# Expert second product as five f32r passes, ternary product in bf16, and five scatters to six gathers

## Chip, core and metric

The kernel runs on one core of a Trainium2 chip (trn2). The metric is the device time of one launch in microseconds. The engines named below: TensorE (PE in the profile), VectorE (DVE), ScalarE (ACT), GpSimd (POOL), and SyncE (SP), which issues most transfers.

## Reference

Eight batches of 288 rows (256 positions and 32 text rows) of 256 numbers go through five stages; each stage after the first adds its result to the rows `h`:

```python
h = tok(x)                                   # AFT-style mixer over positions
h = concat([h, txt], axis=1)                 # (8, 288, 256)
h = h + attention(layernorm(h))              # 8 heads, decayed linear attention, gate
h = h + ffn(layernorm(h), weight)            # ternary weights, 4-bit rows
h = h + agent(layernorm(h), w_qkv, w_conv1)  # one agent row per batch
h = h + experts(layernorm(h), ...)           # 8 experts, top 2, plus a shared one

def ffn(x, weight):
    xh = x @ hadamard                                     # (256, 256)
    s = clip(max(|xh|, axis=-1), 1e-5) / 7
    xq = clip(round(xh / s), -8, 7) * s
    ws = clip(mean(|weight|, axis=1), 1e-5)
    wq = where(weight/ws > .5, 1, where(weight/ws < -.5, -1, 0)) * ws
    return xq @ wq.T

def experts(x, gate_w, W1, W2, Ws1, Ws2):
    scores = softmax(x @ gate_w.T); top_vals, top_idx = top_k(scores, 2)
    y, g = split(x @ W1[e].T)            # W1[e]: (384, 256), halves of 192
    out_e = (y * silu(g)) @ W2[e].T      # W2[e]: (256, 192)
    return sum over the two experts of top_vals * out_e  + the same with Ws1, Ws2
```

## The kernel before

The 8 x 288 rows lie in 18 tiles of 128 rows (`NI`), two for the positions of each batch and two shared tiles for the text of four batches each. They stay in on-chip memory (`hres`). Each engine has its own program, written out by hand; it runs its instructions in order and waits on semaphores that other engines raise. `ge(engine, semaphore, n)` waits only if n is above zero. There is no planner: the order in the code is the order on the engine.

**Attention and ternary stage** (`attention_and_ffn`). The loop `for b in steps` runs b from -2 to 7 on every engine. In one step batch b finishes its attention, batch b+1 starts, and unit u = b-1 (the two tiles of a batch, with a third, a text tile, after every fourth batch) goes through the ternary layer: its rows are normalised, turned, multiplied with the Hadamard matrix (`rotate`), quantised (`quantise`), turned again (`turn_q`), and multiplied with the ternary weights (`ternary`, L1126). The weights were prepared once by `ffn_weights` and `ffn_split` as the sum of two f32r parts with the row scale in them. VectorE's `add` (L1512) then scales the product by the row scale and adds it into `hres` in one operation, and raises `h2_done`. On TensorE the order within a step is: `ternary(u)`, `output(b, 0)`, `denominators(b+1)`, `scores(b+1, 0)`, `spread_out(b+1)` (L1018, the broadcast of the inverted denominators), `output(b, 1)`, and then the next scores. `spread_out(b+1)` waits for the inverted denominators (`rd_done`, VectorE) and for `h2_done` of unit u of the same step, since it writes over the banks that held the unit's product. On VectorE the order there is `add(u)`, `rows_sums(b+3)` (the statistics of a later batch), `invert(b+1)`, a mask, `divide(b+1)`. On GpSimd it is, among others, `rows_root(b+3)` (L616, L619; only for b up to 4). The last three tiles are units of their own after the loop (`parts`).

**Expert stage** (`mixture`). Rows are normalised and stored to `x_rows` in HBM; the shared expert's first four groups of rows, the gate, the choice of two experts and the numbering of the rows come first. VectorE builds one-hot tables (`one_hot`, L2629), TensorE turns them into source rows (`find`), VectorE writes the row indices (`sources`) and the expert of each block (`expert_of_block`). Then follow `take(2)` and `gated(11)` on VectorE, `shared_output(3)` on TensorE (L2278), and the loop over 43 blocks of 128 rows (`NB`). For block j GpSimd gathers the rows (L2816, an indirect DMA of 128 rows), TensorE turns them (`turn_rows`, L2311), ScalarE and VectorE split them into two f32r parts, TensorE makes the first product (`hidden`, six matrix products, L670 to L672), ScalarE and VectorE gate it, TensorE turns it (`turn`, L2331), ScalarE copies it out, TensorE makes the second product (`second`, L2340, f32 with 96 rows of contraction, twice), ScalarE copies the result into an output buffer (L2534), and GpSimd scatters it to `y_rows` (L2824). In iteration j TensorE's order is `hidden(j)`, `turn_rows(j+2)`, `second(j-2)`, `turn(j-1)`. GpSimd's order is gather(j), scatter(j-8); a gather waits until the block four before has been turned, and an output buffer is free again when the scatter four before has landed. After the loop, and after all scatters, SyncE fetches the rows back, VectorE adds them with their weights (`combine`, L2667), the shared expert's last two groups are done between, and the rows are stored.

Of the kernel before, what the change touches and what calls it, by code (L numbers as in the profile page):

```python
# [25 lines left out]
P = 128  # L26
B, F, L, H0 = 8, 64, 256, 4
TXT = 32
D = 256
# [646 lines left out]
def attention_and_ffn(nc, g, ins):  # L676
# [5 lines left out]
    with ExitStack() as ctx:  # L682
# [59 lines left out]
        q_t = sb("c_q_t", [P, NT * D], F32R)  # L742
# [5 lines left out]
        wrow = qm[:, 2, :]  # L748
# [3 lines left out]
        tern_t = wf  # L752
# [7 lines left out]
        had, tw_hi, tw_lo = (g["ffw"][:, i] for i in range(3))  # L760
# [32 lines left out]
        tern_ready = sem("b_tern_ready")  # L793
        tern_turned = sem("b_tern_turned")
        rows_read = sem("b_rows_read")
        ternt_ready = sem("b_ternt_ready")
# [143 lines left out]
        def _(pe):  # L940
# [68 lines left out]
            def spread_out(b):  # L1009
                pe.wait_ge(gate_read, 2 * (b + 1))  # L1010
                pe.wait_ge(rd_done, b + 1)
                if b == 0:
                    pe.wait_ge(rows_read, 2)
# [63 lines left out]
            def ffn_weights():  # L1077

                pe.wait_ge(tern_ready, 1)
# [13 lines left out]
            def turn_unit(u):  # L1093
                pe.wait_ge(f_xn_done, u + 1)
                if u == 0:
                    pe.wait_ge(rows_read, 2)
# [110 lines left out]
        def _(act):  # L1207
# [80 lines left out]
            for b in steps:  # L1288
# [40 lines left out]
                if b == -1:  # L1329
                    act.wait_ge(tern_turned, 1)  # L1330
                    nc.scalar.copy(tern_t, ps[:, 2, :].bitcast(BF16)[:, 0:FC * D].rearrange(
                        "p (c f) -> p c f", c=FC)).then_inc(ternt_ready, 1)
                    act.wait_ge(tern_turned, 2)
                    nc.scalar.copy(wrow, ps[:, 3, 0:D]).then_inc(rows_read, 1)
# [22 lines left out]
        def _(dve):  # L1357
# [85 lines left out]
            def ffn_weights():  # L1443
# [18 lines left out]
                last.then_inc(tern_ready, 1)  # L1462
# [1519 lines left out]
```

## Time and profile before

| | us |
|---|---|
| three runs | 625.04, 627.95, 628.0 |
| median | 627.95 |
| profiled execution | 625.87 |
| its span, first to last instruction | 624.1 |

| engine | busy us | share of the span |
|---|---|---|
| TensorE, products | 549.2 | 88% |
| VectorE | 408.5 | 65% |
| ScalarE | 279.2 | 45% |
| GpSimd | 228.6 | 37% |

The attention and ternary stage takes from about 125 to 382 us, the expert stage the rest, its loop over blocks from about 480 to 587. A time in the rows below counts from the first instruction of the profiled execution. Busy time of a TensorE row overlaps with that of its neighbours, as products are pipelined; the distance from start to start is what one costs.

### The profile page before, as it was taken

Reading aid. Unit: us, or ns where it says so; the run is one execution under the profiler, and the core shown is the slowest. Engines: PE = TensorE matmul, PEld = TensorE weight load, DVE = VectorE, ACT = ScalarE, POOL = GpSimd, SP = SyncE. Lnnn points to the kernel's source line nnn. Section 1 sums busy time; section 2 is a strip of 40 time slices with the busy share of each in tenths; the row PEclk is TensorE's granted clock in tenths of the full one; section 3 lists DMA queues with packets and bytes.
Section 4 is the critical chain, followed back from the end, with each engine's and each line's share of the span. In section 5 each row is a group of like instructions: output and inputs, shape, how many; then the busy total and the mean of one; then the engine's idle time right before and its main releaser. Section 6 shows DMA issues by size and latency. Waiting matters only on the chain. (4 is left out here: it accounts for less than half of the span.)

```text
span 624.1 us, 11683 instructions
## 1 busy us (share of the span) xinstructions
PE 549.2 (88%) x4038; PEld 475.5 (76%) x4038; DVE 408.5 (65%) x1034; ACT 279.2 (45%) x590; POOL 228.6 (37%) x342
## 2 busy tenths in 40 slices
PE   5899948799999999999999776798897999999983
PEld 4799837688898989898988553566786999988862
DVE  2498975758788887898888866645674332222166
ACT  1543334525455565565564343736311555554300
POOL 2367781501121211212112115751014777777300
PEclk9999967889999999999999987679998999999977
DMA  6312113000000000000000703202001333333267
GB/s 220 99 51 68 34 52 101 1 1 2 2 1 2 2 1 2 2 1 2 3 1 1 254 1 103 75 27 77 1 2 50 101 104 102 103 103 109 97 202 216
DMA packets 27444, 37.03 MB, mean 59 GB/s; under 512 B 4541, under 2 KB 22782, under 8 KB 27390
## 3 DMA queue, kind: packets, MB, share of 16 engines
q1 hardware_dynamic: 23166, 24.78, 12.9%
q0 software_dynamic: 4224, 11.54, 6.0%
q8 instruction: 33, 0.54, 0.4%
q14 instruction: 21, 0.17, 0.1%
HBM read 25.95 MB, written 10.35 MB: 58 GB/s over the span
## 5 line engine op out<-in xcount | busy, mean ns | idle before, releaser
L2747 DVE TENSOR_TENSOR w1raw<-ps,w1raw 128x192 f32<-128x192 f32 x43 | 15.4, 358 | 69.0 <-ACT w1raw L2527 69.0
L670 PE MATMUL ps<-b_x_hi,wa_hi 128*128 128x288 f32 x192 | 57.7, 301 | 0.5 <-PEq L104 0.5
L671 PE MATMUL ps<-b_x_lo,wa_hi 128*128 128x288 f32 x192 | 57.3, 298 | 0.0
L672 PE MATMUL ps<-b_x_hi,wa_lo 128*128 128x288 f32 x192 | 57.1, 297 | 0.0
L1641 POOL TENSOR_TENSOR c_rstd<-c_ve,mhalf 128x2 f32<-128x2 f32 (+2 forms) x20 | 13.5, 676 | 112.4 <-DVE c_ve L564 112.4
L2816 POOL DMA_INDIRECT kv<-x_rows,r_src_i x43 | 41.8, 972 | 27.1 <-issue 10.4
L1708 POOL TENSOR_TENSOR w1raw<-w1raw 128x288 f32<-128x288 f32 x16 | 16.6, 1057 | 80.5 <-DVE w1raw L1399 80.5
L2340 PE MATMUL ps<-w,w1raw 96*128 x172 | 44.6, 381 | 1.3 <-ACT w1raw L2539 1.3
L1393 DVE TENSOR_TENSOR w1raw<-ps,decay 128x960 f32<-128x960 f32 x32 | 36.8, 1151 | 7.8 <-PE ps L1036 6.0
L1036 PE MATMUL ps<-w1raw 64*128 64x160 f32 (+2 forms) x384 | 38.3, 342 | 0.9 <-DVE w1raw L1424 0.9
L670 PEld LDWEIGHTS ps<-b_x_hi,wa_hi 128*128 128x128 f32 x192 | 36.6, 191 | 1.3 <-issue 0.9
L1036 PEld LDWEIGHTS ps<-w1raw 64*128 64x128 f32 x384 | 32.1, 198 | 6.8 <-DVE w1raw L1424 1.1
L671 PEld LDWEIGHTS ps<-b_x_lo,wa_hi 128*128 128x128 f32 x192 | 36.7, 191 | 0.4
L672 PEld LDWEIGHTS ps<-b_x_hi,wa_lo 128*128 128x128 f32 x192 | 36.7, 191 | 0.0
L1399 DVE SCALAR_TENSOR_TENSOR w1raw<-b_ex,w1raw 128x576 f32<-128x576 f32 x32 | 25.1, 784 | 14.6 <-ACT w1raw L1219 14.3
L284 PE MATMUL ps<-a_nk,a_ewt 128*128 128x256 f32 (+1 forms) x128 | 32.4, 400 | 2.5 <-ACT a_eq L362 2.5
L670 PE MATMUL ps<-w_hi,f_w 128*128 x86 | 32.7, 380 | 0.8 <-DVE f_w L2657 0.8
L1261 ACT ACTIVATE c_xn<-hres,c_shift,c_rstd 128x256 f32<-128x256 f32 x18 | 9.9, 594 | 51.4 <-POOL c_shift L1650 51.4
L2340 PEld LDWEIGHTS ps<-w,w1raw 96*128 96x128 f32 x172 | 29.3, 189 | 4.4 <-issue 2.1
L670 PE MATMUL ps<-d_x,w_hi 128*128 128x384 f32 x72 | 26.8, 372 | 5.3 <-DVE x L2572 5.3
L1052 PE MATMUL ps<-w1raw,b_v 128*64 128x288 f32 (+1 forms) x256 | 30.4, 363 | 1.0 <-DVE b_yt L1379 0.4
L1215 ACT ACTIVATE b_ex<-ps 128x576 f32<-128x576 f32 x32 | 20.9, 654 | 22.3 <-PE ps L672 22.3
(390 smaller groups left out, 1626.5 us busy)
## 6 DMA issues: line engine op xcount, KB each, us to landing
d_x<-y_rows SPq DMA_DIRECT2D x18, 256.0 KB, 4.1
w1raw<-in_W_t SPq DMA_DIRECT2D x8, 384.0 KB, 6.2
x_rows<-w1raw SPq DMA_DIRECT2D x6, 384.0 KB, 2.6
a_xt<-in_x_t SPq DMA_DIRECT2D x8, 256.0 KB, 3.5
a_xfl<-in_x_flat SPq DMA_DIRECT2D x8, 256.0 KB, 2.8
out<-hres SPq DMA_DIRECT2D x16, 128.0 KB, 3.9
w<-in_W_t SPq DMA_DIRECT2D x8, 192.0 KB, 4.5
w1raw<-in_Ws_t SPq DMA_DIRECT2D x1, 768.0 KB, 9.9
```

Source lines behind the costliest of these rows:

```text
L284: mm = nc.tensor.matmul(ps[:, 4 + part, t * D:(t + 1) * D], ewt[:, s, t * P:(t + 1) * P], nk[:, b % 2, s, part * D:(part + 1) * D], start= ...
L670: nc.tensor.matmul(out, x_hi, w_hi, start=start, stop=False)
L671: nc.tensor.matmul(out, x_hi, w_lo, start=False, stop=False)
L672: return nc.tensor.matmul(out, x_lo, w_hi, start=False, stop=stop)
L1036: mm = nc.tensor.matmul(ps[:, bank(j) + r, col:col + n], held[rows, keys], qk[rows, NP + j, T - n:T], start=True, stop=True)
L1052: mm = nc.tensor.matmul(ps[DK * r:DK * r + DK, 6 + j % 2, T - n:T], rows[:, h * DK:(h + 1) * DK], a[:, j % 2, r, col:col + n], start=s == ...
L1215: nc.scalar.activation(ex[:, i % 2], ps[:, group(i):group(i) + 2, 0:T], ACT.Exp)
L1393: nc.vector.tensor_tensor(a[:, j % 2], ps[:, bank(j):bank(j) + 2, 0:AW], g["decay"][:, 2 * j:2 * j + 2, :], ALU.mult).then_inc(masked, 1)
L1399: nc.vector.scalar_tensor_tensor(out=qk[:, qk_tiles(i), 0:T], in0=ex[:, i % 2], scalar=1.0, in1=qk[:, qk_tiles(i), 0:T], op0=ALU.min, op1= ...
L1708: nc.gpsimd.tensor_tensor(z[:, j, :], z[:, j, :], qk[:, NP + j, 0:T], ALU.mult).then_inc(qz_done, 1)
L2340: mm = nc.tensor.matmul(ps[:, 6 + u, 0:D], e_ht[:, u, k, :], w2[:, k, bass.ds(e, 1), :].rearrange("p a f -> p (a f)"), start=k == 0, stop= ...
L2816: pool.indirect_dma_start(xg[j % NX], None, x_rows, bass.IndirectOffsetOnAxis(ap=src_i[:, j:j + 1], axis=0)).then_inc(gathered[j % NX], 16)
```

## The change

In the ternary layer the weights stay as they are, -1, 0 and 1, in bf16 (`tern_t`), and the quantised rows are bf16 as well, so that `ternary` has two products for each tile instead of four. The scale of the weights (`wrow`) is applied afterwards: VectorE multiplies the product by both scales into `qm`, and an operation of its own adds that to `hres`: on GpSimd for the units in the loop (`add_unit`, put after `rows_root` in GpSimd's step), on VectorE for the last three tiles (`add_part`). `ffn_split` loses three VectorE operations. `h2_done` is raised by the add.

In the expert stage W2 lies in one block of 128 rows and one of 64 twice, and is split into two f32r parts: ScalarE rounds (`round_w2`, four operations of 128x1024, ahead of `row_part`), VectorE subtracts for the second block (`split_w2`, four of 128x512, ahead of `take(2)`), GpSimd for the first (four of 128x512, one ahead of `tile_part` and three behind it). The turned rows are split likewise in the loop (`split_hidden`), and the second product is five f32r products. `turn(j-1)` moves ahead of `turn_rows(j+2)`. There are six gather buffers instead of four, and fourteen output buffers instead of four, whose scatters are waited for in groups of seven. GpSimd issues its first scatter after the twelfth gather, then five scatters to six gathers, and the rest at the end. W2 is loaded by three transfers instead of eight.

```diff
-        q_t = sb("c_q_t", [P, NT * D], F32R)
+        q_t = sb("c_q_t", [P, NT * D], BF16)
...
             def ternary(u):
...
-                        for k, w in enumerate((tw_hi, tw_lo)):
-                            mm = nc.tensor.matmul(tile_rows(u)[:, t, :], of_unit(q_t, u)[:, fc, t * P:(t + 1) * P],
-                                                  w[:, fc, :], start=fc + k == 0, stop=fc + k == 2)
+                        mm = nc.tensor.matmul(tile_rows(u)[:, t, :], of_unit(q_t, u)[:, fc, t * P:(t + 1) * P],
+                                              tern_t[:, fc, :], start=fc == 0, stop=fc == FC - 1)
...
             def scaled_rows(u):
                 act.wait_ge(inv_done, u + 1)
+                ge(act, h2_done, whole_units(u))
...
             def ffn_split():
                 nc.vector.tensor_copy(had, hraw)
-                dve.wait_ge(rows_read, 2)
-                dve.wait_ge(ternt_ready, 1)
-                step = Steps(dve, ternt_ready, 1)
-                step(nc.vector.tensor_tensor(tern_t, tern_t, wrow.rearrange(
-                    "p (a f) -> p a f", a=1).to_broadcast([P, FC, D]), ALU.mult))
-                step(nc.vector.tensor_copy(tw_hi, tern_t))
-                nc.vector.tensor_tensor(tw_lo, tern_t, tw_hi.bitcast(F32), ALU.subtract)
+                dve.wait_ge(rows_read, 3)
...
             def add(u):
                 dve.wait_ge(ff_done, u + 1)
-                for t, i in enumerate(unit(u)):
-                    r = hres[:, i, :]
-                    last = nc.vector.scalar_tensor_tensor(out=r, in0=tile_rows(u)[:, t, :],
-                                                          scalar=xsc[:, slots(u)][:, t:t + 1], in1=r,
-                                                          op0=ALU.mult, op1=ALU.add)
-                last.then_inc(h2_done, 1)
+                for t in range(len(unit(u))):
+                    last = nc.vector.scalar_tensor_tensor(out=qm[:, slots(u)][:, t, :], in0=tile_rows(u)[:, t, :],
+                                                          scalar=xsc[:, slots(u)][:, t:t + 1], in1=wrow[:],
+                                                          op0=ALU.mult, op1=ALU.mult)
+                last.then_inc(scaled_back, 1)
+
+            def add_part(u):
+                dve.wait_ge(scaled_back, u + 1)
+                r = hres[:, unit(u)[0], :]
+                nc.vector.tensor_tensor(r, qm[:, slots(u)][:, 0, :], r, ALU.add).then_inc(h2_done, 1)
...
             for u in parts:
                 add(u)
+                add_part(u)
                 agent_norm_sums(u)
...
+            def add_unit(u):
+                pool.wait_ge(scaled_back, u + 1)
+                r = hres[:, 2 * u:2 * u + 2, :]
+                last = nc.gpsimd.tensor_tensor(r, qm[:, 0:2, :], r, ALU.add)
+                if ends(u):
+                    r = hres[:, text_tile(u), :]
+                    last = nc.gpsimd.tensor_tensor(r, qm[:, 2, :], r, ALU.add)
+                last.then_inc(h2_done, 1)
...
                 if 2 <= b + 3 < B:
                     rows_root(nc, g, pool, b + 3)
+                if is_unit(u):
+                    add_unit(u)
...
-        NX, NY, NG = 4, 4, 5
-        LAG = 8
+        NX, NY, NG = 6, 14, 5
+        GROUP = NY // 2
+        LAG = 10
...
             def second(j, e):
                 u = j % 2
-                pe.wait_ge(ht_done, j + 1)
+                pe.wait_ge(ht_lo_done, j + 1)
                 ge(pe, yo_done, j - 1)
-                for k in range(2):
-                    mm = nc.tensor.matmul(ps[:, 6 + u, 0:D], e_ht[:, u, k, :],
-                                          w2[:, k, bass.ds(e, 1), :].rearrange("p a f -> p (a f)"),
-                                          start=k == 0, stop=k == 1)
+                if j == 0:
+                    pe.wait_ge(w_rounded, NGR + 1 + 4 + 8)
+                first, rest = ht_hi[:, u, 0:P], ht_hi[:, u, P:2 * P]
+                for n, (rows, w, c) in enumerate(((first, w2_hi, 0), (first, w2_lo, 0), (ht_lo[:, u, :], w2_hi, 0),
+                                                  (rest, w2_hi, 1), (rest, w2_lo, 1))):
+                    mm = nc.tensor.matmul(ps[:, 6 + u, 0:D], rows,
+                                          w[:, c, bass.ds(e, 1), :].rearrange("p a f -> p (a f)"),
+                                          start=n == 0, stop=n == 4)
...
+            def round_w2():
+                act.wait_ge(later_in, 16 * 4)
+                act.wait_ge(w_rounded, NGR + 1)
+                act.wait_ge(sh_done, 2 * 9)
+                for c in range(2):
+                    for e in range(0, E, 4):
+                        nc.scalar.copy(w2_hi[:, c, e:e + 4, :], w2_raw[:, c, e:e + 4, :]).then_inc(w_rounded, 1)
...
-                    ge(act, y_stored[u], 16 * ((j - 2) // NY))
+                    ge(act, y_stored[u // GROUP], 16 * GROUP * ((j - 2) // NY))
...
+            def split_w2():
+                dve.wait_ge(w_rounded, NGR + 1 + 4)
+                for e in range(0, E, 2):
+                    V.tensor_tensor(w2_lo[:, 1, e:e + 2, :], w2_raw[:, 1, e:e + 2, :],
+                                    w2_hi[:, 1, e:e + 2, :].bitcast(F32), ALU.subtract).then_inc(w_rounded, 1)
+
+            def split_hidden(j):
+                u = j % 2
+                dve.wait_ge(ht_done, j + 1)
+                V.tensor_tensor(ht_lo[:, u, :], ps[:, 4 + u, 0:P], ht_hi[:, u, 0:P].bitcast(F32), ALU.subtract)
+                V.tensor_tensor(ht_hi[HB2:P, u, P:2 * P], ps[HB2:P, 4 + u, P:2 * P],
+                                ht_hi[HB2:P, u, P:2 * P].bitcast(F32), ALU.subtract).then_inc(ht_lo_done, 1)
...
             expert_of_block()
+            split_w2()
             take(2)
             gated(11)
...
+            pool.wait_ge(w_rounded, NGR + 1 + 4)
+            split_w2(0)
             tile_part()
+            for e in range(2, E, 2):
+                split_w2(e)
...
-            for j in range(NB + LAG):
-                if j < NB:
-                    gather(j)
-                if j >= LAG:
-                    scatter(j - LAG)
+            for j in range(NB):
+                gather(j)
+                for n in range(scattered(j - 1), scattered(j)):
+                    scatter(n)
+            for n in range(scattered(NB - 1), NB):
+                scatter(n)
```

In the last loop `scattered(j)` is `max(0, (j - LAG + 1) * 5 // 6)`.

## Rows read from the trace of the kernel before

**Rows 1.** Busy time of the engines in two stretches: PE, PEld, DVE, ACT, POOL, clock, DMA

```profile
125.00:360.00 235.00, 226.20 (x2261) 200.89 (x2262) 196.33 (x461) 124.73 (x232) 42.20 (x73) 0.99 0.05 18
500.00:560.00 60.00, 60.00 (x358) 54.91 (x357) 17.33 (x51) 31.00 (x100) 45.69 (x47) 1.00 0.33 104
```

**Rows 2.** Chain that ended last: start, us, what; second products 24 blocks apart

```profile
485.08 0.87 PE ps L2340 x4
...
541.76 0.88 PE ps L2340 x4
```

**Rows 3.** Timeline of POOL in the expert loop: start, us, instruction, idle before it

```profile
479.99 0.95 POOL L2816 DMA_INDIRECT kv<-x_rows,r_src_i  x1 [5.33 <-PE ps L2311]
...
543.29 0.99 POOL L2824 DMA_INDIRECT y_rows<-e_junk,r_dst_i  x1 [0.30 <-ACT kv L2534]
...
545.86 0.99 POOL L2824 DMA_INDIRECT y_rows<-f_ub,r_dst_i  x1 [0.30 <-issue]
...
587.16 0.97 POOL L2824 DMA_INDIRECT y_rows<-e_junk,r_dst_i  x1 [1.05 <-ACT e_junk L2534]
```

**Rows 4.** Timeline of PE: a ternary product of two tiles and what follows

```profile
237.53 1.12 PE L1126 MATMUL ps<-f_w,c_q_t 128*128 128x256 f32 x8
238.49 0.28 PE L670 MATMUL ps<-b_wo_hi,b_y_hi 128*128 128x256 f32 x1
```

**Rows 5.** Timeline of PE: the last shared output before the loop

```profile
473.66 1.84 PE L2278 MATMUL ps<-ws,x 128*128 128x256 f32 x4 [3.00 <-DVE d_ht_last L2572]
```

**Rows 6.** Timeline of DVE: the subtraction in the weight split

```profile
149.52 0.69 DVE L1476 TENSOR_TENSOR f_w<-c_xn,f_w 128x512 fp32r<-128x512 f32 x1
```

**Rows 7.** Timeline of POOL: the tile part

```profile
457.98 2.79 POOL L2811 TENSOR_TENSOR w1raw<-w1raw,r_tile_no 128x1548 bf16<-128x1548 bf16 x1 [30.29 <-DVE w1raw L2624]
```

**Rows 8.** Timeline of DVE: the one-hot tables

```profile
461.83 5.29 DVE L2629 TENSOR_TENSOR x<-w1raw,r_row 128x768 bf16<-128x768 f32 x6
```

**Rows 9.** Timeline of DVE: one instruction at two places

```profile
268.07 1.02 DVE L1527 CUSTOM_DVE_ANT_0 wo<-x,f_ub 128x256 f32<-128x256 f32 x1
...
374.27 0.42 DVE L1527 CUSTOM_DVE_ANT_0 wo<-x,f_ub 128x256 f32<-128x256 f32 x1
```

**Rows 10.** Timeline of POOL at the first of these places

```profile
267.77 1.99 POOL L1708 TENSOR_TENSOR w1raw<-w1raw 128x288 f32<-128x288 f32 x2 [8.48 <-DVE w1raw L1399]
```

**Rows 11.** Groups by line, POOL: count, busy us, mean ns, idle before

```profile
L495 POOL TENSOR_TENSOR a_hn<-a_hn,a_lng 128x512 f32<-128x512 f32 x7 | 8.9, 1271 | 1.7 <-ACT a_hn L368 1.7
```

**Rows 12.** Timeline of ACT: the row part

```profile
457.93 1.60 ACT L2458 ACTIVATE w1raw<-w1raw,r_row_no 128x1548 bf16<-128x1548 bf16 x1 [7.72 <-DVE w1raw L2624]
```

**Rows 13.** Timeline of POOL: the end of the root in four steps

```profile
181.87 0.19 POOL L619 TENSOR_TENSOR b_shift<-b_nmu,b_rstd 128x3 f32<-128x3 f32 x1
...
211.22 0.20 POOL L619 TENSOR_TENSOR b_shift<-b_nmu,b_rstd 128x2 f32<-128x2 f32 x1
...
241.67 0.20 POOL L619 TENSOR_TENSOR b_shift<-b_nmu,b_rstd 128x2 f32<-128x2 f32 x1
...
275.03 0.20 POOL L619 TENSOR_TENSOR b_shift<-b_nmu,b_rstd 128x2 f32<-128x2 f32 x1
```

**Rows 14.** Timeline of PE: the broadcast in the same steps

```profile
181.70 1.13 PE L1018 MATMUL ps<-b_rd,b_spread 32*128 32x72 f32 x32 [0.24 <-issue]
...
211.31 1.13 PE L1018 MATMUL ps<-b_rd,b_spread 32*128 32x72 f32 x32
...
241.75 1.13 PE L1018 MATMUL ps<-b_rd,b_spread 32*128 32x72 f32 x32
...
275.02 1.13 PE L1018 MATMUL ps<-b_rd,b_spread 32*128 32x72 f32 x32 [0.22 <-issue]
```

**Rows 15.** Timeline of PE: the broadcast in the step of the weight split

```profile
152.35 1.13 PE L1018 MATMUL ps<-b_rd,b_spread 32*128 32x72 f32 x32 [1.15 <-DVE b_rd L1418]
```

**Rows 16.** Groups by line, DVE: an addition of one tile

```profile
L1431 DVE TENSOR_TENSOR hres<-ps,hres 128x256 f32<-128x256 f32 x16 | 6.1, 419 | 0.7
```

**Rows 17.** Timeline of DVE: the first of the last three tiles

```profile
375.17 0.48 DVE L1512 SCALAR_TENSOR_TENSOR hres<-ps,c_xsc,hres 128x256 f32<-128x256 f32 x1
```

More of the change, by code:

```diff
@@ L759, in attention_and_ffn @@
         w1c = sb("b_w1c", [P, FC])
-        had, tw_hi, tw_lo = (g["ffw"][:, i] for i in range(3))
+        had = g["ffw"][:, 0]
+        tern_t = sb("b_tern_t", [P, FC, D], BF16)
+        wrow = sb("b_wrow", [P, D])
         identb, ub, roundc = g["identb"], g["ub"], g["roundc"]
@@ L1461, in ffn_weights @@
                                                           in1=tneg[:, c, :], op0=ALU.is_gt, op1=ALU.subtract)
-                last.then_inc(tern_ready, 1)
+                last.then_inc(prep, 1)
                 for c in range(FC):
@@ L2077, in mixture @@
         old = g["x3"][:].rearrange("p i f -> p (i f)")
-        s_ht_rows = old[:, 0:2 * NC * TP - TP].rearrange("p (n r) -> p n r", r=TP)
-        s_ht_last = sb("d_ht_last", [P, TP])
+        s_ht_rows = old[:, 0:2 * NC * TP].rearrange("p (n r) -> p n r", r=TP)
         sct = sb("d_sct", [E, TP])
@@ L2121, in mixture @@
         xg = [tiles[:, u, :] for u in range(NX)]
-        yo = [tiles[:, NX, :], tiles[:, NX + 1, :], g["e"][1]["junk"][:, 1, :], g["ub"][:]]
+        yo = [old[:, 2 * NC * TP + u * D:2 * NC * TP + (u + 1) * D] for u in range(9)]
+        yo += [g["e"][1]["junk"][:, u, :] for u in range(4)] + [g["ub"][:]]
         split = g["ffw"][:].rearrange("p a c d -> p (a c) d")
@@ L2126, in mixture @@
         hg = held["hg"].rearrange("p (u h) -> p u h", u=2)
-        e_ht = held["e_ht"][0:HE // 2].rearrange("p (u k m) -> p u k m", u=2, k=2)
+        flat = xs[0][:].rearrange("p b s c r -> p (b s c r)")
+        w2_hi = flat[:, 0:2 * E * D].rearrange("p (c e f) -> p c e f", c=2, e=E)
+        ht_hi = flat[:, 2 * E * D:2 * E * D + 4 * P].rearrange("p (u m) -> p u m", u=2)
+        ht_lo = sb("f_ht_lo", [P, 2, P], F32R)
         yg = xs[0][:].bitcast(F32).rearrange("p b s c r -> p (b s c r)")[:, 0:NG * 2 * D].rearrange("p (u k f) -> p u k f", u=NG, k=2)
@@ L2156, in mixture @@
         gathered = [sem(f"f_gathered{u}") for u in range(NX)]
-        y_stored = [sem(f"f_y_stored{u}") for u in range(NY)]
+        y_stored = [sem(f"f_y_stored{u}") for u in range(2)]
         e_turned = sem("f_x_turned")
@@ L2182, in s_ht @@
         def s_ht(b, i):
-            return s_ht_last[:] if b % 2 and i == NC - 1 else s_ht_rows[:, NC * (b % 2) + i, :]
+            return s_ht_rows[:, NC * (b % 2) + i, :]
         def pair_of(k):
@@ L2196, in _ @@
             sp.dma_start(g["ws2"][:], ins["Ws2_t"].rearrange("(c p) n -> p c n", p=P)).then_inc(later_in, 16)
-            for e in range(E):
-                sp.dma_start(g["w2"][:, :, e, :],
-                             ins["W2_t"][e].rearrange("(c p) n -> p c n", p=HE // 2)).then_inc(later_in, 16)
+            for rows, c, first in ((slice(0, P), 0, 0), (slice(0, HB2), 1, P), (slice(HB2, P), 1, P)):
+                n = rows.stop - rows.start
+                sp.dma_start(w2_raw[rows, c], ins["W2_t"][:, first:first + n, :].rearrange("e p n -> p e n")
+                             ).then_inc(later_in, 16)
             for b in range(NGR):
@@ L2206, in fetch @@
                 sp.dma_start(yg[:, i % NG], rows[:, i]).then_inc(fetched[i % NG], 16)
-            for u in range(NY):
-                sp.wait_ge(y_stored[u], 16 * ((NB - u + NY - 1) // NY))
+            for u in range(2):
+                sp.wait_ge(y_stored[u], 16 * sum(j // GROUP % 2 == u for j in range(NB)))
             for i in range(NG):
@@ L2403, in _ @@
                     hidden(j, of[j])
+                if 1 <= j <= NB:
+                    turn(j - 1)
                 if j + 2 < NB:
@@ L2411, in _ @@
                     of.append(expert(j + 1))
-                if 1 <= j <= NB:
-                    turn(j - 1)
             pe.wait_ge(hg_done, NB)
-            pe.wait_ge(ht_done, NB)
+            pe.wait_ge(ht_lo_done, NB)
             shared_hidden(NC * FIRST)
@@ L2824, in scatter, with scattered @@
                 pool.indirect_dma_start(y_rows, bass.IndirectOffsetOnAxis(ap=dst_i[:, j:j + 1], axis=0),
-                                        yo[j % NY], None).then_inc(y_stored[j % NY], 16)
+                                        yo[j % NY], None).then_inc(y_stored[j // GROUP % 2], 16)
+            def scattered(j):
+                return max(0, (j - LAG + 1) * 5 // 6)
             def lo_w1(n):
```

56 lines of the change are left out of this document (30 added, 26 removed).

## The prediction

> **What bounds the kernel now.** I read the share of each engine by stretch first, then the chain that ended last, then the timeline of one engine at a time around the edited lines.
>
> From 125 to 360 us, the attention and ternary stage, TensorE is busy for 226.20 of 235 us [rows 1]: what TensorE saves or waits there moves the end, and what another engine does there moves it only where TensorE waits for it. From 500 to 560 us, the expert loop, TensorE is busy without a gap, but GpSimd, which issues every gather and scatter, counts 45.69 of 60 us although issue gaps are not busy time [rows 1]. The chain shows the loop's period on TensorE: the second product starts at 485.08 and, 24 blocks later, at 541.76, so 2.36 us a block [rows 2]. GpSimd's timeline shows the other period: scatter to scatter, with one gather between, is 543.29 to 545.86, 2.57 us, 1.285 us an issue with the gaps [rows 3]. So GpSimd is already slower than TensorE by 0.21 us a block; it keeps up only by a stock of rows gathered ahead. It is held at the start (the fifth gather waits 5.33 us for TensorE's first transpose) and at the end (the last scatter, at 587.16, waits 1.05 us for its row) [rows 3]. In between lie 82 issues in 107.17 us, where 81 intervals of 1.285 make 104.1: about 3 us of waits in all. That is the floor that counts below.
>
> **Second product.** Now 0.87 us a block, four instructions [rows 2]. The new one is five matrix products in f32r of 256 columns. The nearest row is the ternary product, the same type and size: eight start at 237.53 and the next work at 238.49, 0.12 us each [rows 4]. Five make 0.60; the period falls to 2.09 us. If an f32r pass cost what one of the four old instructions does, 0.22 us, it would be 1.09 and the period 2.58. I take 0.12, the row of the same form. VectorE's added operations (a second gating product, two subtractions) lie beside a period that GpSimd sets. By itself all this is worth nothing, since GpSimd needs 2.57 us a block.
>
> **Gathers ahead, five scatters to six gathers.** Nothing is removed: 43 gathers and 43 scatters are still issued. With six buffers, six gathers instead of four go out before TensorE's first transpose frees one; 80 issues remain instead of 82, and late scatters have stock, so the waits at the end go. After the restart the last scatter starts 79 intervals later, 101.5 us, and I allow 1.0 us for the first blocks, in which TensorE must turn a block before the next gather may go. Fourteen output buffers in two groups of seven make ScalarE wait for scatters of the group before, for some microseconds near blocks 28 and 35; TensorE has 0.48 us a block of slack to absorb that. So the stretch from GpSimd's restart to the last scatter shrinks from 107.2 to 102.5: -4.7 us.
>
> **When that restart comes.** Two edits push it back.
>
> (1) VectorE's four subtractions for the second half of the weights stand ahead of the take and the gating product that TensorE's last shared output waits for (3.00 us at 473.66) [rows 5], and TensorE turns the first gathered rows only after that output. One 128x512 subtraction from SBUF took 0.69 us [rows 6]; four back to back 2.6 us, no cover: +2.6.
>
> (2) GpSimd's three subtractions of 128x512 come after its tile part, which ended at 460.77 [rows 7], so they run where VectorE builds the one-hot tables, 5.29 us from 461.83 [rows 8], on the path to the source indices and the first gather. One VectorE instruction took 0.42 us at 374.27 with GpSimd idle, and 1.02 us at 268.07 beside a GpSimd product [rows 9, 10]: 0.41 of its speed. Three GpSimd operations at 1.27 us [rows 11] overlap for 3.8 us, which costs 0.59 x 3.8 = 2.3 us. If GpSimd is stretched too (its pair took 1.99 us for 2 x 288 columns, where 1.27 x 288/512 gives 0.71 each, so 1.39 times), it is 3.1; if the one-hot form is indifferent, 0. I take +2.3, as the slowed row also reads two operands from SBUF.
>
> The Trainium skill says the same of the mechanism (GPSIMD Engine Reference, section 8, Key points): GpSimd shares its SBUF interfaces with VectorE and collides with VectorE instructions that have two SBUF inputs. It speaks against this placement; the 0.42 and 1.02 agree. By that rule the +2.3 stands, without it the term is nothing.
>
> ScalarE's four roundings of the weights fit into its 7.72 us of idle time before 457.93 [rows 12]; if that cover went, they would delay the same tables. So the restart moves from 479.99 to 484.9, and the last scatter to 484.9 + 102.5 = 587.4 against 587.16: the expert stage as a whole, +0.2 us.
>
> **Ternary product and the add.** Each tile needs two passes instead of four: 0.24 us less, 0.48 for a unit of two tiles. But the result now goes VectorE (scaling, the same operation as before) and then GpSimd (add), and TensorE's broadcast of the denominators still waits for the end of the add. GpSimd works in program order, and its add stands after the root of the batch three ahead. That root exists in four steps, and its last instruction ends at 182.06, 211.42, 241.87 and 275.23 [rows 13], while the broadcasts start at 181.70, 211.31, 241.75 and 275.02 [rows 14]: there is no slack to put an add into. A 128x512 GpSimd add took 1.27 us [rows 11], and the fourth of these units has a third tile, 0.64 more. Moved earlier by the 0.48 saved, then the add: broadcasts at 182.85, 212.21, 242.66, 276.66, so +1.15 + 0.90 + 0.91 + 1.64 = +4.6. TensorE's queue is in order: the next output product and the next scores stand behind that wait, so the loss is not made up while TensorE is 96% busy. With the slowed GpSimd rate (1.39 times) it would be +6.8; no stall and only the saving would be -1.9. The three other two-tile units have no root ahead of the add; there I take nothing, between -0.5 and +0.3 each.
>
> Removing the weight split takes three operations of up to 0.69 us [rows 6] from VectorE in the first step, where TensorE waits 1.15 us for the reciprocal behind it [rows 15]: -1.15; what then is late is TensorE's own scores.
>
> For the last three tiles the add stays on VectorE as an operation of its own, 0.42 us by the like addition of 128x256 [rows 16]. VectorE works through these tiles without idling from 375.17 on [rows 17] and the ending of the stage hangs on it: 3 x 0.42 = +1.3.
>
> **Sum.** +4.6 - 1.15 + 1.3 + 0.2 = +4.9 us. The profiled execution took 625.87 us (span 624.1), 2.1 below the median of 627.95; the three runs lie between 625.04 and 628.0. From the profiled one the sum gives 630.8, from the median 632.9; I forecast between them, **631.8 us**.
>
> **Rivals.**
> *No collision.* The one-hot tables build at their old pace, as their broadcast operands might load less. Then +2.6: about 629.5. For it: no row shows this form beside GpSimd arithmetic; against: the small two-operand products at 268 us. Chance 0.25.
> *Faster.* GpSimd's gap of 0.30 us between issues is a wait that the deeper buffers remove, not its own cost. Then an issue takes 0.98 us, TensorE sets the pace, and 45 periods of 2.09 us from 484.9 put the last scatter near 579, 8 us earlier; the sum is 4.7 - 8.2 = -3.5: about 623.4. It decides once a pair costs less than TensorE's 2.09 us. Against it: 0.30 stands between issues long after their data is ready [rows 3]. Chance 0.13.
> *Slower still.* Both collisions at the stretched price: the adds cost +2.2 and the tables +0.8 more; with a longer TensorE pause before the loop, near 635.5. Chance 0.13.
> *The five passes are no cheaper* (0.22 us each): TensorE's 2.58 us a block equals GpSimd's pair and its waits return, near 635 too. Chance 0.04.
> The forecast has 0.45, its own range 630 to 634.
>
> **Numbers.** The measurement tells a change from none at about 0.5%, 3.1 us: 624.8 to 631.1. Faster: the faster rival and a little, 0.15. Same: most of no collision and a third of the forecast, 0.36. Slower: the rest, 0.49. The range that leaves two in ten out is 624.5 to 636.5.
>
> **What would show it.** Right: the four broadcasts wait 1.3 to 2 us, with GpSimd's add as the releaser; the one-hot row grows from 5.29 to over 7 us; the second product is near 0.6 us; GpSimd issues without a pause at 1.285 us from about 485 to the last scatter at about 587, and TensorE's chain has gaps in the loop instead. Wrong: broadcasts on time, issue gaps under 0.3 us, or a last scatter well before 584.

## The result, and the profile after

The changed kernel takes 634.68 us (median of four runs, 633.52 to 636.29) against 627.0 us (four runs, 625.04 to 628.0): ratio 1.0128, interval 1.0089 to 1.0168. Run again beside the experiments it was 635.72 against 624.14, ratio 1.0185, interval 1.0149 to 1.022. It is slower, by 7.7 us in the first series and 11.6 in the second, and the intervals of both ratios lie above 1; the forecast was 631.8, in a range from 624.5 to 636.5. The profiled execution took 636.29 us, 10.4 above the profiled one of before.

Every stage lies between events that exist in both traces, so their distances can be set against the terms of the forecast. The third column is a second profile of the same kernel, from the second series.

| from ... to ..., us | before | changed | again | forecast |
|---|---|---|---|---|
| broadcast of the step of the weight split to the one with three tiles (152.35 to 275.02 before) | 122.67 | 129.24 | 127.64 | +4.6 |
| to the last broadcast | 58.13 | 57.81 | 59.32 | 0 |
| to the first one-hot table | 128.68 | 132.80 | 130.33 | +1.3 |
| the six tables | 5.29 | 8.49 | 8.50 | +2.3 |
| to the last shared output | 6.54 | 9.56 | 9.06 | +2.6 |
| to GpSimd's restart | 6.33 | 7.14 | 7.16 | 0 |
| to the last scatter | 107.17 | 103.02 | 102.95 | -4.7 |
| to the end of the last store's issue | 35.43 | 34.00 | 34.20 | 0 |

The first event itself comes 1.42 us earlier, and its wait of 1.15 us is gone [rows 15]. In the second profile the wait is gone too, but the event comes 0.50 us later than before, as the broadcast ahead of it already comes 2.82 us later. The sums from there are +11.8 and +8.9.

The four broadcasts in TensorE's timeline after (start, us, what, idle time before it and what ended it) answer to [rows 14]:

```profile
181.52 1.13 PE L1017 MATMUL ps<-b_rd,b_spread 32*128 32x72 f32 x32 [1.66 <-POOL hres L1661]
213.66 1.13 PE L1017 MATMUL ps<-b_rd,b_spread 32*128 32x72 f32 x32 [1.11 <-POOL hres L1661]
245.07 1.13 PE L1017 MATMUL ps<-b_rd,b_spread 32*128 32x72 f32 x32 [1.10 <-POOL hres L1661]
280.17 1.13 PE L1017 MATMUL ps<-b_rd,b_spread 32*128 32x72 f32 x32 [2.61 <-POOL hres L1664]
```

All four wait, and GpSimd's add is the releaser. GpSimd's timeline at the first of them shows the order that does it [rows 13]:

```profile
179.00 0.88 POOL L616 TENSOR_TENSOR b_rstd<-b_ve,mhalf 128x3 f32<-128x3 f32 x1 [3.42 <-DVE b_ve L564]
179.96 0.19 POOL L619 TENSOR_TENSOR b_shift<-b_nmu,b_rstd 128x3 f32<-128x3 f32 x1
180.11 1.26 POOL L1661 TENSOR_TENSOR hres<-c_qm,hres 128x512 f32<-128x512 f32 x1
```

GpSimd sits idle for 3.42 us ahead of the root; the add, whose input had been ready since 177.3, starts only behind it and ends 0.15 us before the broadcast.

Busy time by stretch (PE, PEld, DVE, ACT, POOL, clock, DMA) answers to [rows 1] and adds two stretches:

```profile
125.00:360.00 235.00, 223.27 (x2198) 195.00 (x2198) 188.88 (x429) 123.87 (x230) 49.31 (x78) 0.97 0.04 14
183.40:186.60 3.20, 3.20 (x18) 2.70 (x18) 1.56 (x4) 0.00 (x0) 0.00 (x0) 0.50 0.00 0
477.20:493.20 16.00, 11.91 (x45) 9.68 (x44) 9.45 (x27) 0.49 (x1) 6.07 (x6) 0.50 0.17 49
500.00:560.00 60.00, 59.80 (x416) 57.91 (x417) 40.23 (x144) 34.19 (x111) 44.59 (x46) 1.00 0.33 102
```

From 183.4 to 186.6 the granted clock is 0.50, the lower level of 1.2 GHz, right behind the first of the waits. In the same stretch before, it stayed at 1.00:

```profile
183.40:186.60 3.20, 3.20 (x35) 2.83 (x36) 2.74 (x5) 0.28 (x1) 0.00 (x0) 1.00 0.00 0
```

From 477.2 to 493.2 it is at the lower level too, where TensorE waits for the tables and for VectorE.

VectorE after, the tables [rows 8] and its part of the weight split; GpSimd after, its part of the split, the restart and the last scatter [rows 3]:

```profile
470.78 8.49 DVE L2657 TENSOR_TENSOR x<-w1raw,r_row 128x768 bf16<-128x768 f32 x6
...
484.79 2.53 DVE L2691 TENSOR_TENSOR w<-w,d_x 128x512 fp32r<-128x512 f32 x4
```

```profile
470.69 5.15 POOL L2859 TENSOR_TENSOR w<-w,d_x 128x512 fp32r<-128x512 f32 x3
...
495.97 0.95 POOL L2864 DMA_INDIRECT kv<-x_rows,r_src_i  x1 [5.93 <-PE ps L2328]
...
598.99 0.97 POOL L2872 DMA_INDIRECT y_rows<-x,r_dst_i  x1 [0.30 <-issue]
```

TensorE after, the last shared output [rows 5], and second products of two blocks in turn [rows 2], from two answers:

```profile
488.83 6.64 PE L2295 MATMUL ps<-ws,x 128*128 128x256 f32 x18 [3.62 <-DVE x L2600]
```

```profile
514.73 0.36 PE L2360 MATMUL ps<-d_x 128*128 x1
514.93 0.28 PE L2360 MATMUL ps<-w,d_x 128*128 x1
...
515.41 0.34 PE L670 MATMUL ps<-w_hi,f_w 128*128 x1
...
516.82 0.36 PE L2360 MATMUL ps<-d_x 128*128 x1
```

The second product takes 0.68 us from 514.73 to 515.41 (the first pass 0.20, each further one 0.12), the block 2.09 us, where nothing is waited for.

### The profile page after: what moved, and what is told of

The parts are those of the page before. It is cut to its first block and busy times, and to the rows that moved or that the text cites. A ratio compares the mean times of both kernels' runs of the same rounds, so it can differ in the third digit from the quotient of the medians.

```text
span 634.5 us, 11926 instructions
## 1 busy us (share of the span) xinstructions
PE 547.4 (86%) x4045; PEld 474.0 (75%) x4045; DVE 444.1 (70%) x1167; ACT 282.8 (45%) x594; POOL 244.0 (38%) x354
## 5 line engine op out<-in xcount | busy, mean ns | idle before, releaser
L2295 PE MATMUL ps<-ws,x 128*128 128x256 f32 x108 | 29.1, 431 | 5.1 <-DVE x L2600 5.0
L670 PE MATMUL ps<-w_hi,f_w 128*128 x86 | 31.4, 365 | 1.9 <-issue 1.0
L2295 PEld LDWEIGHTS ps<-ws,x 128*128 128x128 f32 x108 | 23.3, 220 | 10.2 <-DVE x L2600 6.4
L2872 POOL DMA_INDIRECT y_rows<-x,r_dst_i x28 | 27.6, 985 | 8.5 <-issue 7.9
```

The costliest lines, as they stand in the source:

```text
L670: nc.tensor.matmul(out, x_hi, w_hi, start=start, stop=False)
L2295: mm = nc.tensor.matmul(ps[:, 6 + t // 2, (t % 2) * D:(t % 2) * D + D], s_ht(b, i)[:, t * P:t * P + P], ws2[:, i, :], start=i == 0, stop=i ...
L2872: pool.indirect_dma_start(y_rows, bass.IndirectOffsetOnAxis(ap=dst_i[:, j:j + 1], axis=0), yo[j % NY], None).then_inc(y_stored[j // GROUP ...
```

## The experiments

Theory: the change loses its time in three separate places where an added operation stands ahead of one that TensorE waits for; what the loop gains is GpSimd's order of issues, not the shorter product. The rivals stand with each run.

**The changed kernel again.** No edit.

> The changed kernel itself, once more. Theory (the cost is in waits that the program's order makes): the four broadcasts wait 1.1 to 2.6 us for GpSimd's add again, the one-hot tables take 8.3 to 8.7 us, GpSimd's restart to its last scatter takes 103 us, and the ratio to the kernel before is 1.010 to 1.016. Rival (part of the 7.7 us was chance in TensorE's clock): the stretches at half clock at 183 to 187, 354 to 366 and 477 to 493 us are not all there again, and the ratio is under 1.010.

Waits of 1.65, 1.10, 1.11 and 2.62 us, tables 8.50, restart to last scatter 102.95: as expected. The ratio is above the upper end, and the intervals of the two series overlap. The stretch at half clock behind the waits was there again, at another wait, the fourth:

```profile
281.20:284.40 3.20, 3.20 (x28) 3.07 (x24) 1.42 (x2) 0.00 (x0) 0.00 (x0) 0.50 0.03 5
```

So its place was chance and its presence not: each of the seven profiles with these waits has at least one such stretch between 131 and 346 us, and none of the seven profiles without them (the kernel before among them) has any.

**The add ahead of the root.**

```diff
+                if is_unit(u):
+                    add_unit(u)
                 if 2 <= b + 3 < B:
                     rows_root(nc, g, pool, b + 3)
-                if is_unit(u):
-                    add_unit(u)
```

> GpSimd's add of a unit stands ahead of the root of the batch three ahead instead of behind it; nothing else. Theory (queue order on GpSimd): the add starts as soon as VectorE has scaled the product, 2.7 us earlier, and ends before the inverted denominators are ready; the four waits of 1.66, 1.11, 1.10 and 2.61 us go, and 6.5 to 8.5 us with them: 626 to 628 us. Rival (collision): the add now runs beside VectorE's statistics of the rows and slows them to 0.4 of their speed, so that the inverted denominators are late instead: at most 3.5 us gained, 631 us or more. Rival (TensorE is ahead anyway and the time comes back at the agent rows): under 2 us gained.

628.23 us, 7.5 less than the changed kernel, as expected, though the time is 0.2 above the range given; ratio to the kernel before 1.0046 (1.0023 to 1.0068). TensorE, GpSimd and VectorE of this run, and its clock over all the steps:

```profile
274.28 1.13 PE L1017 MATMUL ps<-b_rd,b_spread 32*128 32x72 f32 x32 [0.58 <-DVE b_rd L1417]
```

```profile
179.14 1.29 POOL L1661 TENSOR_TENSOR hres<-c_qm,hres 128x512 f32<-128x512 f32 x1 [1.80 <-DVE c_qm L1504]
```

```profile
178.97 1.07 DVE L556 BATCH_NORM_STATS2 b_stats<-hres 128x6 f32<-128x256 f32 x3
```

```profile
131.00:348.00 217.00, 212.09 (x2150) 186.66 (x2146) 183.54 (x411) 121.61 (x224) 48.56 (x75) 1.00 0.02 6
```

Only the fourth broadcast still waits, 0.58 us, and now for VectorE. The statistics beside the add keep their 1.07 us, so the collision rival falls. The first stretch of the table is 121.57 us, 1.1 below before: with the waits gone, the shorter ternary product seems to be worth something (no run isolates it).

**GpSimd's three subtractions behind its sixth gather.**

```diff
             tile_part()
-            for e in range(2, E, 2):
-                split_w2(e)
...
                 gather(j)
+                if j == NX - 1:
+                    for e in range(2, E, 2):
+                        split_w2(e)
```

> GpSimd's last three subtractions of the W2 split come after its sixth gather, in its wait for TensorE's first turned block (5.93 us), instead of behind the tile part; nothing else. Theory (collision with VectorE's tables): the one-hot tables fall from 8.49 to 5.3 us, the first gather comes 3.2 to 3.5 us earlier, TensorE's pause there and its half clock get shorter, and the three subtractions fit into GpSimd's wait: 3.2 to 4.4 us gained, 630.3 to 631.5 us. Rival (the tables are slow for another reason, such as ScalarE beside them): tables stay over 8 us and the time within 1 us. Rival (the subtractions overrun GpSimd's wait): the fifth gather to follow them starts late and the gain is under 1.5 us.

631.86 us, 3.9 less: the gain lies inside what was expected, the time 0.4 above. VectorE's tables and GpSimd's subtractions:

```profile
470.28 5.29 DVE L2657 TENSOR_TENSOR x<-w1raw,r_row 128x768 bf16<-128x768 f32 x6
```

```profile
485.80 3.71 POOL L2859 TENSOR_TENSOR w<-w,d_x 128x512 fp32r<-128x512 f32 x3
```

Apart, the tables have their old price, 5.29 us, and the subtractions take 1.24 us each; together they took 8.49 and 1.72 each.

**VectorE's four subtractions behind the last gating product.**

```diff
             expert_of_block()
-            split_w2()
             take(2)
             gated(11)
+            split_w2()
```

> VectorE's four subtractions of the W2 split come behind the take and the last gating product instead of ahead of them; nothing else. Theory (they stand on the path to TensorE's last shared output): that output starts 2.5 us earlier, the subtractions lie in the 7.36 us in which VectorE idles before the first block, and the time falls by 2.3 to 2.6 us to about 632.2 us. Rival (TensorE's product ahead of it, at half clock, ends as late as the subtractions): under 0.7 us gained. Rival (moved behind, they hold back the split of the first turned rows): no gain.

632.36 us, 3.4 less, above the upper end of what was expected, though the runs spread from 628.16 to 636.1.

```profile
487.15 5.64 PE L2295 MATMUL ps<-ws,x 128*128 128x256 f32 x18 [3.00 <-DVE x L2600]
```

First gather to last shared output is 3.95 us as before (6.45 in the changed kernel's second profile), so 2.5 came from there; the shared output itself takes 1.0 less, because TensorE pauses 3.00 us instead of 5.52 and runs less of it at the lower level. In this profile the tables took only 7.13 us, as they began later beside GpSimd's subtractions; that is not the move's doing.

**The three together.**

> The three moves together: the add ahead of the root, GpSimd's last three subtractions after the sixth gather, VectorE's four behind the last gating product. Theory (three separate waits on one path, each paid once): the gains of 7.5, 3.9 and 2.5 us add up; the fourth broadcast comes 121.6 us after the first, the tables take 5.3 us, first gather to last shared output 3.9 us, and the time is 621 to 622.5 us, so at least 1.5 us below the kernel before. Rival (they share one clock loss, which only one of them can give back): 624 us or more, no faster than before.

619.83 us, 1.2 below the range expected; ratio to the kernel before 0.9908 (0.9877 to 0.9939). The gains add up (14.1 us from the first broadcast of the table to the end, against the changed kernel's second profile, where 7.5, 3.9 and 2.5 were expected): the waits were paid one behind the other. By the medians, each set against the kernel before of its own series, it is 17.8 us (from +11.6 to -6.2), some 3 us more than the three single gains of 7.5, 3.9 and 3.4; the intervals leave about that much open. This version beats both kernels.

**Only one half of the change.** First the changed expert stage with the old ternary part, then the other way round.

```diff
-                        mm = nc.tensor.matmul(tile_rows(u)[:, t, :], of_unit(q_t, u)[:, fc, t * P:(t + 1) * P],
-                                              tern_t[:, fc, :], start=fc == 0, stop=fc == FC - 1)
+                        for k, w in enumerate((tw_hi, tw_lo)):
+                            mm = nc.tensor.matmul(tile_rows(u)[:, t, :], of_unit(q_t, u)[:, fc, t * P:(t + 1) * P],
+                                                  w[:, fc, :], start=fc + k == 0, stop=fc + k == 2)
...
```

> Only the expert stage is the changed one; the ternary product, its weights and the fused add are those of before. Theory: its balance is +3.2 (tables), +2.5 (VectorE's subtractions), +0.8 (last shared output at half clock), -4.2 (loop), -1.2 (rows behind the last scatter), so 1 us slower than before: 624 to 626.5 us, and the stretch from the last broadcast to the last of the three single tiles is 42.6 us as before. Rival (the lower clock between 350 and 415 us comes from the expert stage's new loads, not from the ternary part): that stretch stays at 44 to 46 us and the time is 627 us or more.

> Only the ternary part is the changed one; the expert stage is that of before. Theory: the whole loss of the waits and what follows them is here, 5 to 8 us up to the last single tile and nothing behind: 630 to 633 us. Rival (the ternary part alone costs the 4.8 us that were forecast for it, and the rest of the loss belongs to the expert stage): 628 to 629.5 us.

The expert stage alone: 625.95 us, ratio 1.0003 (0.9973 to 1.0033). From the last broadcast to the last single tile it took 46.29 us, as the rival said, but the next stretch gave it back, and from the last broadcast to the tables it is 127.97, 0.7 below before; the rival's price was not paid. The ternary part alone: 631.76 us, ratio 1.0098 (1.006 to 1.0135). Its profiled execution, 628.18 us, is the shortest of its six; in it, from the table's first broadcast to its last 186.93 us against 180.80, so 6.1 us of waits with what follows them, and 1.4 up to the tables. So the loss that can be measured is in the ternary half; in the expert half losses and gains cancel. The two halves together make 1.0%, the whole change 1.3% in the first series and 1.9% in the second: in the second some 5 us stand in neither half, and that stays open.

**Three more passes in each second product.**

```diff
+                for c, w in ((0, w2_hi), (1, w2_hi), (1, w2_lo)):
+                    nc.tensor.matmul(ps[:, 6 + u, 0:D], (first, rest)[c],
+                                     w[:, c, bass.ds(e, 1), :].rearrange("p a f -> p (a f)"), start=True, stop=True)
```

> The changed kernel with three more matrix products of the same size in each second product (three of the five done once before, then overwritten): 0.36 us more TensorE work in a block. Theory (GpSimd's issues set the loop's pace at 2.57 us a block, TensorE has 0.48 us to spare): a block takes TensorE 2.45 us, the stretch from GpSimd's restart to the last scatter stays at 103 to 104.5 us, and the time within 1.5 us of the changed kernel, about 635.7 us. Rival (TensorE's second product sets the pace of the loop): 43 x 0.36 = 15 us slower, 650 us.

641.76 us, 6.0 more than the changed kernel (4.1 more when each is set against the kernel before of its own series): more than the theory allowed, and far less than the rival's 15. GpSimd's timeline:

```profile
519.47 0.94 POOL L2867 DMA_INDIRECT kv<-x_rows,r_src_i  x1 [0.84 <-PE ps L2328]
...
534.15 0.94 POOL L2867 DMA_INDIRECT kv<-x_rows,r_src_i  x1 [0.89 <-PE ps L2328]
...
603.97 0.97 POOL L2875 DMA_INDIRECT y_rows<-x,r_dst_i  x1 [0.30 <-issue]
```

The gather now waits for TensorE once in six blocks (14.68 us, 2.45 a block). My limit of 2.57 was wrong: with five scatters to six gathers GpSimd needs eleven issues for six blocks, 11 x 1.285 / 6 = 2.36 us a block. From the first turned block to the last scatter it is 108.31 against 103.61.

**The old second product in the new loop.** The three moves stay; `second`, `turn`, the layout of W2 and the gating are those of before, and all splitting of W2 and of the turned rows is gone.

```diff
-                for n, (rows, w, c) in enumerate(((first, w2_hi, 0), (first, w2_lo, 0), (ht_lo[:, u, :], w2_hi, 0),
-                                                  (rest, w2_hi, 1), (rest, w2_lo, 1))):
...
+                for k in range(2):
+                    mm = nc.tensor.matmul(ps[:, 6 + u, 0:D], e_ht[:, u, k, :],
...
-                    round_w2()
...
-            split_w2()
...
-                    split_hidden(j - 1)
```

> The three moves, the six gather and fourteen output buffers and the five-to-six order stay, but the second product is that of before (four f32 instructions, 2.36 us a block on TensorE), and so the whole split of W2 and of the turned rows is gone. Theory (GpSimd's order made the loop shorter; eleven issues of 1.285 us for six blocks are 2.36 us a block, so TensorE at 2.36 is just not late): from the eight passes, 108.3 us at 2.45, 43 x 0.09 less gives 104.4 us from the first turned block to the last scatter against 103.6, and the time is within 1.5 us of that of the three moves, 619.8 us. Rival (the shorter second product made the loop shorter): 107 to 108 us as before, and 623 to 624.5 us.

619.48 us, ratio 0.9916 (0.9887 to 0.9945): the same as with five passes. TensorE's period is 2.35 us (second products at 516.44 and 518.79), and the stretch from the first turned block to the last scatter is 104.06 us, against 107.82 before and 103.61 in the changed kernel. So 3.8 of the loop's 4.2 us come from the buffers and the order (which of the two, no run separates), and 0.4 from the five passes.

**Two blocks turned ahead of the last shared output**, first with five passes, then with the old second product. Both stand on the three moves; in the first, GpSimd's three subtractions come after its eighth gather.

```diff
-            shared_output(3)
-
             pe.wait_ge(idx_done, 3)
             turn_rows(0)
             of = [expert(0)]
             turn_rows(1)
+            shared_output(3)
```

> The three moves, and TensorE turns the rows of the first two blocks ahead of its last shared output, in the 3.9 us that it waits there for VectorE; GpSimd's three subtractions come after its eighth gather. Theory (GpSimd's pause before the seventh gather starts the whole chain of issues): that gather comes 2.5 us earlier, TensorE's first product follows the shared output at once, and the last scatter comes 1 to 2.5 us earlier: 617.5 to 619 us. Rival (TensorE then waits for the first gathered rows and for the block's expert, and its shared output comes late): no gain or up to 1 us slower, 620 to 621 us.

619.59 us, ratio 0.9909 (0.988 to 0.9938): no gain. The shared output does come later, as the rival said, 4.46 us after the first gather instead of 3.95, but that is not what sets the end. GpSimd's issues (to the eighth gather, then the ninth, then the last scatter):

```profile
469.24 1.15 POOL L2863 DMA_INDIRECT kv<-x_rows,r_src_i  x1 [7.92 <-DVE r_src_i L2675]
...
478.68 0.94 POOL L2863 DMA_INDIRECT kv<-x_rows,r_src_i  x1 [0.30 <-issue]
483.57 0.97 POOL L2863 DMA_INDIRECT kv<-x_rows,r_src_i  x1 [0.16 <-issue]
...
582.14 0.97 POOL L2871 DMA_INDIRECT y_rows<-x,r_dst_i  x1 [0.30 <-issue]
```

From first gather to last scatter are 112.90 us: 85 intervals of 1.28 and the 3.78 us of the subtractions, nothing else. GpSimd has no pause left to give up.

> The second product of before in the new loop (as in the run with the old second product), and TensorE turns the first two blocks ahead of its last shared output. Theory (with five passes GpSimd had no pause left, so an earlier start of TensorE bought nothing; with the old product at 2.36 us a block TensorE sets the end, so an earlier start arrives there): GpSimd's pause of 2.8 us before its seventh gather goes, the last scatter comes 1.0 to 1.6 us earlier than without the move, 112.1 to 112.7 us after the first gather instead of 113.7, and the time is 617.5 to 619 us. Rival (GpSimd's issues are the limit here too): 113.3 us or more from the first gather, and no gain.

616.92 us, ratio 0.9894 (0.9861 to 0.9927): the lowest of all and 0.6 below the range expected, though its interval overlaps those of the runs above. First gather to last scatter is 112.63 us against 113.69 without the move, inside the expected 112.1 to 112.7: here TensorE set the end, and its earlier start arrives there.

**GpSimd's subtractions as copies of one input.** The low part of the first block of W2 is left out.

```diff
-                nc.gpsimd.tensor_tensor(w2_lo[:, 0, e:e + 2, :], w2_raw[:, 0, e:e + 2, :],
-                                        w2_hi[:, 0, e:e + 2, :].bitcast(F32), ALU.subtract).then_inc(w_rounded, 1)
+                nc.gpsimd.tensor_copy(w2_lo[:, 0, e:e + 2, :], w2_hi[:, 0, e:e + 2, :].bitcast(F32)
+                                      ).then_inc(w_rounded, 1)
```

> The changed kernel with GpSimd's four subtractions as plain copies of one input of the same size (the low part of the first block of W2 is left out, the rounded weights are copied there instead). Theory (VectorE's form with two operands from on-chip memory gives way to whatever GpSimd does there): the tables stay slow in proportion to the time that the copies run beside them, at 0.4 of their speed. Rival (it is GpSimd's second input that collides): the tables take 5.3 to 6.0 us.

One execution, 631.01 us. VectorE's tables, and GpSimd's three copies:

```profile
468.62 5.96 DVE L2657 TENSOR_TENSOR x<-w1raw,r_row 128x768 bf16<-128x768 f32 x6
```

```profile
467.84 2.45 POOL L2859 CAST w<-d_x 128x512 fp32r<-128x512 f32 x3
```

The copies end at 470.29, so 1.67 us of the tables lie beside them, and 0.67 us are lost: 0.60 of the old speed. Beside the subtractions it was 0.37: 5.06 us (470.78 to 475.84), 3.20 lost. In the run with VectorE's subtractions moved, where the tables came later against GpSimd's three, 2.84 us lay beside them and 1.84 were lost, 0.35.

These shares hide what happens. One instruction at a time, GpSimd and VectorE in the changed kernel:

```profile
470.69 1.27 POOL L2859 TENSOR_TENSOR w<-w,d_x 128x512 fp32r<-128x512 f32 x1
470.78 2.00 DVE L2657 TENSOR_TENSOR x<-w1raw,r_row 128x768 bf16<-128x768 f32 x1
471.93 1.98 POOL L2859 TENSOR_TENSOR w<-w,d_x 128x512 fp32r<-128x512 f32 x1
472.70 2.02 DVE L2657 TENSOR_TENSOR x<-w1raw,r_row 128x768 bf16<-128x768 f32 x1
473.87 1.98 POOL L2859 TENSOR_TENSOR w<-w,d_x 128x512 fp32r<-128x512 f32 x1
474.65 2.01 DVE L2657 TENSOR_TENSOR x<-w1raw,r_row 128x768 bf16<-128x768 f32 x1
```

and with the copies:

```profile
468.40 0.61 POOL L2859 CAST w<-d_x 128x512 fp32r<-128x512 f32 x1
468.62 1.20 DVE L2657 TENSOR_TENSOR x<-w1raw,r_row 128x768 bf16<-128x768 f32 x1
468.96 1.33 POOL L2859 CAST w<-d_x 128x512 fp32r<-128x512 f32 x1
469.74 1.36 DVE L2657 TENSOR_TENSOR x<-w1raw,r_row 128x768 bf16<-128x768 f32 x1
```

Whole instructions take turns. Each table ends 0.81 us behind the GpSimd instruction that ran when it began (471.97 to 472.78, and 469.01 to 469.82 beside the copies), and the next GpSimd instruction ends about its own length behind the table: 1.13 us for a subtraction, 0.47 for a copy. So a copy with one input holds a table up as a subtraction with two does, for as long as it lasts, and it costs less because it is shorter (0.56 against 1.25 us from start to start). The tables' 5.96 us lie in the rival's range, but its reason, the second input, falls, and so does the theory's fixed speed of 0.4.

## Why the prediction was right, and where it was not

*Ternary waits, forecast +4.6.* The place, the releaser and the queue order were right, and moving the add took 7.5 us away. By the second profile the four waits alone cost +5.0. Not in the sum was TensorE's clock: behind one of the waits it falls to the lower level for some 3 us of dense products, worth 1.6 us more in the first profile (+6.6); in the second it fell behind the fourth wait and shows as +1.2 in the next stretch.

*Weight split, -1.15.* The wait is gone, and from the broadcast ahead of it this one comes 1.36 us sooner in the first profile (28.72 against 30.08). *Last three tiles, +1.3.* From the first to the last scaling of the three tiles it is 3.57 us with the three moves against 2.65 before, 0.46 for each tile, three of them 1.4.

*Tables, +2.3.* The collision was real, at 0.37 of the speed where I took 0.41, and GpSimd's operations were stretched to 1.72 us, which I had as the upper end, 3.1: it was 3.2. I had taken the middle though [rows 10] showed the stretched GpSimd as well. The Trainium skill (SBUF — State Buffer, SBUF: two separate sides) calls the shared pair of ports an exclusive lock, held for a whole instruction, against a VectorE operation with two SBUF inputs. By that, as an estimate, the tables would end after 5.29 + 3.71 = 9.0 us, all work in a row; 8.49 was measured. The trace agrees on the kind: whole instructions take turns, with some 0.1 us of overlap at each change. It agrees too that the statistics, with one SBUF input, lost nothing beside the add. What the prediction read as a speed of 0.41 was such a turn: the 1.02 us from 268.07 [rows 9] end 0.29 us behind the first of the two GpSimd products [rows 10], which ended at 268.80.

*VectorE's subtractions ahead of the last gating, +2.6.* They took 2.53 us and cost 2.5. Not in the sum: TensorE, which pauses longer for tables and subtractions, runs the last shared output at the lower level, +0.8.

*Loop, -4.7 from the restart.* Measured -4.2, GpSimd issuing at 1.28 us to the end, as forecast, but for three issues of 1.5 to 2.2 us near the start, 1.8 us in all where 1.0 was allowed (103.0 against 102.5). That the shorter product is worth almost nothing held (0.4 us). The reason given did not: the new order lowers GpSimd's need to 2.36 us a block, so TensorE's slack in it is 0.27 us, not 0.48, and three passes more cost 4.7 us.

The mis-sized terms are thus the tables (0.9 too low) and TensorE's clock behind the new waits and pauses (counted as nothing, some 2 us: 1.6 and 0.8 in the first profile, 1.2 and 0.8 in the second). The sum was +4.9, and the two profiles lie 10.4 and 9.4 us above the one before. That the time still fell into the range was in part luck: the forecast stood on 625.9 to 627.95 us for the kernel before, whose median was 623.8 to 626.0 in the later series. What stays open is the stretch from the last broadcast to the tables beyond the three adds, +0.3 to +2.7: the clock falls there at different times in every profile, in kernels with the old ternary part too, and no run isolates why. Open too are the 1.2 to 1.4 us by which the stretch behind the last scatter got shorter, which the sum had at nothing.

## What to carry to other kernels

An operation moved to a less busy engine costs that engine's queue order, not its duration: look at what stands ahead of it in the queue and who waits behind it; here the same add cost 7.5 us more in one place than in the place just above it. Weight preparation on GpSimd belongs where the profile shows VectorE idle as well, or busy with operations of one SBUF input, as the statistics are; where the two collide, each VectorE instruction waits for the GpSimd instruction beside it, so count those. When a loop alternates two kinds of issues on one engine, recompute its need per block from the new ratio before saying which engine has slack, and then ask whether the expensive half of the change is needed at all: the order and the buffers gave nearly all of the loop's gain.

## What the hardware showed unexpectedly

A pause of TensorE of only 1.65 or 2.6 us, between stretches in which it was busy throughout, was followed by the lower clock in seven profiles of seven, behind the first or the fourth of the four waits, once behind both. VectorE's operation with two inputs from SBUF took turns with GpSimd's, whole instruction by whole instruction: 2.0 us each instead of 0.95 beside subtractions of 1.27 us, and 1.20 and 1.36 us beside copies of 0.61, though a copy has one input.
